# Gate and up as seven block products by halves of the tokens, in a gated cross-attention and FFN kernel

## The reference, cut to what matters

```python
x = x + tanh(g_xattn) * xattn(layernorm(x), ctx)          # 32 heads, 8 K/V groups, head size 16
h = layernorm(x)                                          # 2048 tokens x 512
g, u = h @ gate.T, h @ up.T                               # 2048 shared and 256 routed rows each
shared = (g * sigmoid(g) * u)[:, :2048] @ sh_down.T
routed = (g * sigmoid(g) * u)[:, 2048:] @ r_down.T * comb_w   # comb_w: softmax over the two best of 8 logits
x = x + tanh(g_ffn) * (shared + routed)
```

## Time and profile before

| | |
|---|---|
| median of 3 runs | 1016.08 us |
| the profiled execution | 1011.93 us |
| its span | 1010.2 us, so 1.7 us lie around it |
| granted TensorE clock, mean | 0.971 |
| busy in the span | PE 959.4, DVE 518.2, ACT 317.2, POOL 139.6 us |
| attention up to the first FFN product | 0 to 404.69 us |
| FFN | 404.69 us to the end |

### The profile page before, as it was taken

The page is one execution under the profiler, slowest core; times in us unless marked ns, Lnnn a source line. Parts: engine busy times, 40 slices in busy tenths (PEclk is TensorE's granted clock), DMA queues, the critical chain, the costliest instruction groups (busy, mean ns, idle before and its releaser), DMA issues.

```text
span 1010.2 us, 14045 instructions
## 1 busy us (share of the span) xinstructions
PE 959.4 (95%) x5108; PEld 745.0 (74%) x5108; DVE 518.2 (51%) x876; ACT 317.2 (31%) x587; POOL 139.6 (14%) x65
## 2 busy tenths in 40 slices
PE   4689999989998798999999999999999999999998
PEld 4556666766675565888888888888888888778887
DVE  7688777768777795542424242333324242423333
ACT  5165556547545366531111111011111111102110
POOL 4213001300300310400300203003030030120000
PEclk9789999989998799999999999999999999999999
DMA  7774343434334611100100100001001000000012
GB/s 260 168 147 101 70 112 62 92 74 89 81 82 90 172 33 65 63 1 1 63 0 1 63 1 21 41 0 62 0 0 62 0 0 0 1 1 1 1 56 112
DMA packets 33276, 56.71 MB, mean 56 GB/s; under 512 B 4304, under 2 KB 20176, under 8 KB 31824
## 3 DMA queue, kind: packets, MB, share of 16 engines
q1 hardware_dynamic: 33232, 56.13, 21.2%
HBM read 41.17 MB, written 14.68 MB: 55 GB/s over the span
## 4 chain that ended last, share of the span: by engine, by line
PE 73%; issue 17%; DVE 4%; DMA 3%; POOL 2%; ACT 1%; SPq 0%; POOLq 0%; DVEq 0%; ACTq 0%
PE bank L983 22%; PE bank L984 21%; PE bank L985 21%; PE bank L1058 3%; PE bank L1038 2%; PE bank L1048 2%; DVE mcol L695 1%; PE bank L988 1%; POOL xa L392 1%; DMA q_scr<-qx_l 1%; POOL cx_l L361 1%; PE bank L1274 1%; DMA wfc_raw<-wfc 1%; DMA xa<-x 1%; DMA q_st<-q_scr 0%
## 5 line engine op out<-in xcount | busy, mean ns | idle before, releaser
L950 DVE TENSOR_TENSOR hid<-bank,silu 128x512 f32<-128x512 f32 x72 | 49.8, 692 | 353.3 <-ACT silu L652 353.3
L983 PE MATMUL bank<-x2T_l,w_h 128*128 128x512 f32 x576 | 225.3, 391 | 0.0
L985 PE MATMUL bank<-x2T_h,w_h 128*128 128x512 f32 x576 | 224.6, 390 | 0.0
L984 PE MATMUL bank<-x2T_h,w_l 128*128 128x512 f32 x576 | 224.6, 390 | 0.0
L695 DVE TENSOR_REDUCE mcol<-bank 128x2 f32<-128x512 f32 x256 | 170.3, 679 | 59.4 <-PE bank L1038 58.7
L579 ACT ACTIVATE probs<-bank 128x512 f32<-128x512 f32 x256 | 149.6, 594 | 147.3 <-PE bank L1048 146.6
L652 ACT ACTIVATE silu<-bank 128x512 f32<-128x512 f32 x72 | 43.1, 599 | 482.5 <-PE bank L985 482.5
L1038 PE MATMUL bank<-k_st,q_st 65*128 65x256 f32 x512 | 116.2, 316 | 25.1 <-DMA q_st<-q_scr 14.9
L1038 PEld LDWEIGHTS bank<-k_st,q_st 65*128 65x128 f32 x512 | 95.3, 206 | 58.6 <-issue 21.3
L983 PEld LDWEIGHTS bank<-x2T_l,w_h 128*128 128x128 f32 x576 | 108.5, 188 | 23.8 <-issue 0.8
L984 PEld LDWEIGHTS bank<-x2T_h,w_l 128*128 128x128 f32 x576 | 108.6, 188 | 22.4
(11 more groups left out here) (108 smaller groups left out, 933.5 us busy)
## 6 DMA issues: line engine op xcount, KB each, us to landing
w_raw<-w_ffn SPq DMA_DIRECT2D x9, 1536.0 KB, 6.6
q_st<-q_scr SPq DMA_DIRECT2D x96, 128.0 KB, 3.8
xa<-x SPq DMA_DIRECT2D x4, 1024.0 KB, 8.4
cx_raw<-ctxT SPq DMA_DIRECT2D x16, 256.0 KB, 3.4
q_scr<-qx_h SPq DMA_DIRECT2D x16, 256.0 KB, 2.1
q_scr<-qx_l SPq DMA_DIRECT2D x16, 256.0 KB, 2.5
out<-xa SPq DMA_DIRECT2D x16, 256.0 KB, 2.0
k_st<-k_scr SPq DMA_DIRECT2D x24, 128.0 KB, 3.9
```

Of the source, the lines that this page charges most:

```text
L950: v.tensor_tensor(hid[:, ic, :], bank[2 * ic + 1][:, :], silu[:, ic, :], ALU.mult).then_inc(hid_ok, 1)
L983: mm(out, a_h, b_l, start=start, stop=False)
L984: mm(out, a_l, b_h, start=False, stop=False)
L985: return mm(out, a_h, b_h, start=False, stop=stop)
```

## The change

Gate and up of one chunk of 128 rows are now read as one product of 2 x 2 blocks. The left side has the gate chunk in the first row and the up chunk in the second, each cut into two halves of the 512 inputs (A11, A12 and A22, A21). The right side has the same two halves of the inputs by two runs of 512 tokens. In Winograd's form of Strassen's method this takes seven block products of 128 x 256 by 256 x 512 rather than eight, with sums of blocks of the weights (S1 to S4) and of the tokens (T1 to T4) ahead, and sums of the products behind.

The tokens are done in two halves of 1024; the weights are loaded and split anew for each half. In a half there are 18 chunks (quads), in pairs; G = 0 to 35 counts quads, M = 0 to 17 pairs. In each pair the down products of the pair before (8 tiles, 48 matmuls) stand in the first quad between its fourth and fifth product. PE has 36 x 42 matmuls for gate and up where it had 36 x 48; down is as before, 864.

POOL now makes for every quad the four sums S (128 x 256 each), the cast and the subtraction of seven blocks (128 x 1792), and those of the down weights (128 x 512). In the last block of attention it also makes the T sums and splits the token blocks of the first half. ACT copies the turned tiles to `xs0` there. The second half's tiles are prepared between the halves (`turn`, `x7_high` on ACT, `x7_low` on DVE, `differences` on POOL). DVE makes u2, u3, c22, c21, c12 from PSUM and a tile in SBUF, and `hid0`, `hid1` from two tiles in SBUF.

```diff
+TERMS = {1: (A11, B11), 2: (A12, B21), 3: (S4, B22), 4: (A22, T4), 5: (S1, T1), 6: (S2, T2), 7: (S3, T3)}
@@ POOL
-            def split_w(sc, par):
-                    pool.wait_ge(y_full, TILES * BLOCKS * (sc - 1))
-                g.tensor_copy(w_h[par][:, :], w_raw[:, par, :]).then_inc(ffn_w_hi, 1)
-                g.tensor_tensor(w_l[par][:, :], w_raw[:, par, :], w_h[par]..., ALU.subtract).then_inc(ffn_w_ok, 1)
+            def split_gu(G, f):
...
+                    pool.wait_ge(full[3], G - 1)
+                pool.wait_ge(sums, 4 * G + 4)
+                g.tensor_copy(w_h[f][:, :, :], raw[f][:, 0:7, :]).then_inc(gu_hi, 1)
+                pool.wait_ge(gu_hi, G + 1)
+                g.tensor_tensor(w_l[f][:, :, :], raw[f][:, 0:7, :], w_h[f][:, :, :].bitcast(f32),
+                                ALU.subtract).then_inc(gu_ok, 1)
+            def pair(half, m):
+                split_gu(2 * M + 1, 1)
+                block_sums(2 * M + 2, 0, True)
+                for f in range(2):
+                    split_dn(2 * M + f, f, M)
...
+                split_gu(2 * M + 2, 0)
+                block_sums(2 * M + 3, 1, True)
@@ ACT, in the last block of attention
+                if half == 0 and k >= 2:
+                    act.wait_ge(x7_ok, k // 2)
+                copy(lot.rearrange("p a k -> p (a k)"), source[:, :]).then_inc(x2_cp, 1)
@@ ACT, a quad
+                copy(r1[:, :], bank[0][:, :]).then_inc(r1_ok, 1)
+                high(G - 1, M, 1 - f, 1)
+                nc.scalar.activation(s0[:, :], bank[0][:, :], ACT.Silu).then_inc(s0_ok, 1)
+                high(G, M, f, 0)
+                nc.scalar.activation(s1[:, :], c12[:, :], ACT.Silu).then_inc(s1_ok, 1)
@@ DVE, a quad
+                add(u2[:, :], bank[1], r1).then_inc(u2_ok, 1)
+                h_low(G - 1, 1 - f, 1)
+                dve.wait_ge(full[7], G + 1)
+                add(u3[:, :], bank[1], r1).then_inc(u3_ok, 1)
+                accumulate(half, M - 1, range(HTILES), False)      # first quad of a pair
+                add(c22[:, :], bank[2], u3).then_inc(c22_ok, 1)
+                add(c21[:, :], bank[3], u3).then_inc(c21_ok, 1)
+                v.tensor_tensor(hid0[:, :], c21[:, :], s0[:, :], ALU.mult).then_inc(hid_ok[0], 1)
+                dve.wait_ge(full[3], G + 1)
+                add(c12[:, :], bank[2], u2).then_inc(c12_ok, 1)
+                h_low(G, f, 0)
+                dve.wait_ge(s1_ok, G + 1)
+                v.tensor_tensor(hid1[:, :], c22[:, :], s1[:, :], ALU.mult).then_inc(hid_ok[1], 1)
@@ PE, a quad
+                product(1, f, bank[0], False)
+                product(6, f, bank[1], False)
+                pe.wait_ge(r1_ok, G + 1)
+                product(2, f, bank[0], True)
+                pe.wait_ge(u2_ok, G + 1)
+                product(7, f, bank[1], True)
+                if f == 0 and not is_at(m, 0):
+                    down(half, M - 1)
+                product(5, f, bank[2], False)
+                product(4, f, bank[3], False)
+                pe.wait_ge(c22_ok, G + 1)
+                product(3, f, bank[2], True)
```

More of the change, by code:

```diff
@@ L352, in _ @@
+            for half in range(HALVES):
+                pair(half, 0)
+                with sp.Fori(1, PAIRS - 2) as m:
+                    pair(half, m)
+                pair(half, PAIRS - 2)
+                pair(half, PAIRS - 1)
             sp.wait_ge(stored, 16 * (T // P))
@@ new lines, in x7_high, with pair @@
+            def x7_high(j):
+                act.wait_ge(t_ok, 4 * (TILES + j) + 4)
+                act.wait_ge(full[3], FBLOCKS)
+                hi = x7_h[:, :, :, :].rearrange("p a c q -> p (a c) q")[:, :, j * P:(j + 1) * P]
+                copy(hi, xs[j % 2][:, 1:8, :].rearrange("p a (c q) -> p (a c) q", c=2)).then_inc(x7_hi, 1)
+            def pair(half, m):
+                M = PAIRS * half + m
+                turn = half == 0 and is_at(m, PAIRS - 1)
+                quad(2 * M, M, 0, not is_at(m, 0), turn)
+                quad(2 * M + 1, M, 1, True, turn)
+                if is_at(m, 0):
+                    act.wait_ge(comb_ok, 5 * half + 1)
+                    nc.scalar.activation(comb[:, 1, :], comb[:, 0, :], ACT.Tanh, scale=0.5).then_inc(e_ok, 1)
+                if is_at(m, PAIRS - 1):
+                    high(2 * M + 1, M, 1, 1)
+                if turn:
+                    x7_high(0)
+                    x7_high(1)
+                    for k in range(4, 8):
+                        x2_copy(1, k, bank[TURN_BANKS[k - 4]])
+                        if k == 6:
+                            x7_high(2)
+                    x7_high(3)
@@ L665, in _ @@
+            pairs(act, pair)
         @block.vector
@@ L1279, in logits_turn, with product @@
-            def logits_turn(k):
-                pe.wait_ge(lg_cp, 1)
-                pe.wait_ge(acc_ok, TILES * k + 2)
+            Y = bank[4:8]
+            def product(k, f, to, onto):
+                a, b = TERMS[k]
+                for c in range(2):
+                    w = slice(c * P, (c + 1) * P)
+                    last = three(to[:, :], w_h[f][:, a, w], w_l[f][:, a, w], x7_h[:, b, c, :], x7_l[:, b, c, :],
+                                 not onto and c == 0, c == 1, onto)
+                last.then_inc(full[k], 1)
@@ new lines, in turn, with pair @@
+            def turn():
+                for k, ready in zip(range(4, 8), (u3_ok, s0_ok, c21_ok, c12_ok)):
+                    pe.wait_ge(ready, FBLOCKS)
+                    x2_job(1, k, bank[TURN_BANKS[k - 4]])
+            def pair(half, m):
+                if is_at(m, 0):
+                    pe.wait_ge(x7_ok, TILES * (half + 1))
+                quad(half, m, 0)
+                quad(half, m, 1)
+                if is_at(m, PAIRS - 1):
+                    M = PAIRS * half + m
+                    if half == 0:
+                        pe.wait_ge(x2_cp, HTILES + 4)
+                    down_open(M)
+                    if half == 0:
+                        turn()
+                    down_close(M)
+                    if half == 0:
+                        pe.wait_ge(x2_cp, T // P)
@@ L1315 @@
+            for half in range(HALVES):
+                pair(half, 0)
+                pair(half, 1)
+                with pe.Fori(2, PAIRS - 1) as m:
+                    pair(half, m)
+                pair(half, PAIRS - 1)
 _OUT = (B, S, D)
```

719 lines of the change are left out of this document (429 added, 290 removed).

## The result

| | before | changed |
|---|---|---|
| median | 1014.65 us (4 runs, 1008.13 to 1019.41) | 1186.12 us (4 runs, 1180.24 to 1190.51) |
| ratio | | 1.168, 95% interval 1.162 to 1.174 |
| profiled execution, its span | 1011.93, 1010.2 us | 1180.24, 1178.5 us |
| granted TensorE clock, mean | 0.971 | 0.912 |
| PE busy in the span | 959.4 us | 985.5 us |

What follows compares the result with a forecast made beforehand. PE's count of matmuls was taken to bound the FFN. From the profiled span, 1010.2 - 49 + 9 + 1 + 13 = 984; + 115 + 73 = 1172; + 1.7 around the span = 1174 us, range 985 to 1200.

Steps and rivals of the forecast that it cites:

- fewer matmuls: FFN gate and up on PE: 36 quads lose 6 matmuls each, 216 x 0.2267 = 49.0 us less.
- idle for each quad, u2 the releaser: FFN loop, before product 7: PE waits 3.5 us for DVE's u2 in 33 quads, 115 us.
- clock: FFN loop: PE's clock falls to half speed after each idle, costing 2.2 us, 33 times, 73 us.
- a pair: FFN loop: two quads with their down products take 41 us if the collision occurs in every quad.
- loop stall and clock: FFN loop: PE's idles before product 7 and the clock's falls after them, 115 + 73 us.
- attention's last block: End of attention: POOL's new work, waits and transposes, less a split no longer made there, net +13 us.
- the turn: Between the two token halves: preparing the second half's tiles outlasts the down products, 9 us (5 to 13).
- the end: Very end of the kernel: the last low part is ready later than the covering down matmuls end, 1 us.
- loads: FFN weights loaded twice, 27 MB rather than 14, with DMA queues 8% busy: no cost.
- the opening of the FFN: Start of the FFN loop: the prediction had no term for a wait there.
- hid1: Sign in the FFN quads: DVE's hid1 averages 3 us or more, hid0 and the low parts under 1.5.
- who goes first: FFN quad: POOL's waiting subtraction precedes hid1, 3.5 us idle; rival, DVE first, 999 us, chance 0.22.

Runs made afterwards that it cites:

- experiment 1: The changed kernel, but c21, hid0, c12, its silu and hid1 made in place in PSUM banks, so no quad operation of DVE has two SBUF inputs: 1024.14 us.
- experiment 5: Kernel of experiment 1, second half's roots made behind the third quad's split and that quad's weight load issued earlier: 1012.57 us; roots alone 1012.64 us.
- experiment 3: The changed kernel with POOL's subtraction of 1792 columns cut into seven pieces of 256: 1046.92 us, ratio 1.019.
- experiment 4: The changed kernel with DVE's order alone changed, the low part of hid0 made behind the next quad's u2: 1112.20 us, ratio 1.083.
- experiment 6: Kernel of experiment 5 with DVE, ACT and POOL work reordered around the turn: first kernel 997.82 us; second, with two more order changes, 991.69 us.
- experiment 2: The changed kernel with c12 and its silu kept in PSUM and only hid1 read from a bank, written to SBUF: 1085.08 us, ratio 1.056.

## Why the prediction was right

By its own steps, prediction against the profile of the changed kernel:

| step | predicted | measured |
|---|---|---|
| fewer matmuls | -49.0 us | a pair of 132 matmuls takes 29.92 us in experiment 1, 132 x 0.2267 |
| idle for each quad, u2 the releaser | 33 x 3.5 us | 31 x 3.55 (109.9 us) |
| clock | 2.2 us a quad | 1.6 us |
| a pair | every 41 us | 40.77 us |
| loop stall and clock | 115 + 73 = 188 us | 31 x (40.77 - 29.92) / 2 = 168 us |
| attention's last block | +13 us | +10.2 (first FFN product at 414.88, not 404.69) |
| the turn | 9 us | 14.1 us |
| the end | 1 us | 0.98 us |
| loads | 0 | no wait of PE in the FFN is put down to a load; POOL waited for one for 11.6 us at the opening, where moving it won nothing (experiment 5) |
| the opening of the FFN | not seen | 10.5 us |
| hid1 | 3 us or more, the others under 1.5 | 3.9 in the mean; 1.2 the low parts, 1.0 hid0 |

- **What was right** is the sequence: the quad shown runs as it was worked out, and experiments 1, 3 and 4, each from another side, take most or all of the wait away from hid1. That the total came so near is in part luck, as the errors below show, and the range was so wide that it took in a gain as well.
- **The main choice was who goes first** when both engines wait, with only an operation of 0.24 us to go by the earlier trace rows. It was the operation issued first, at 4 us too. The Trainium skill (SBUF — State Buffer, Who interferes with whom) says "Issue order, not op shape, decides who blocks"; hid1 at 4478 ns behind the subtraction and at 797 ns ahead of it (experiment 4) agree.
- **Slightly off:** the subtraction is recorded as 4.32 rather than 4.05 us because it is issued while it still waits for the low part; undisturbed it takes 3.95 (at 450.78, above).
- **The turn was mis-sized**, 14.1 for 9 (idles of 0.56, 3.17 and 10.40). The last low part for the tokens, taken as at most 2.4 us, took 5.77, behind POOL's subtraction for quad 19. I had the rule and did not apply it to this operation. From the timelines of DVE and PE, the tokens' last two low parts and PE's first product of the second half:

```profile
800.75 2.03 DVE L1149 TENSOR_TENSOR x_l<-xs,x_h 128x1792 fp32r<-128x1792 f32 x1 [1.94 <-ACT x_h L576]
...
807.28 5.77 DVE L1149 TENSOR_TENSOR x_l<-xs,x_h 128x1792 fp32r<-128x1792 f32 x1 [3.19 <-ACT x_h L576]
```

```profile
813.16 0.77 PE L1186 MATMUL bank<-x_l,w_h 128*128 128x512 f32 x1 [10.40 <-issue]
```

- **The opening was missed.** The prediction counted what POOL does there, and not what POOL waits for: 9.12 us for DVE's statistics, ahead of a split that is due. The forecast of 1172 for the span came out only 6.5 below 1178.5, because the errors partly cancel: loop 20 and attention 3 too high, turn 5 and opening 10.5 too low, and nothing was put down for the clock behind those two, 2.2 us at the opening and 5.4 at the turn (from the matmuls at half speed there). Some 6 us are not accounted for. The attention's 3 is itself the difference of two executions, and the table above shows how far these differ.
- **A condition that was too narrow.** I wrote of operations with two SBUF inputs. Two of 8 columns, the first in the kernel of experiment 1, the second in the first one of experiment 6, show more (timelines of DVE):

```profile
677.36 3.96 DVE L1096 TENSOR_SCALAR comb<-comb 128x8 f32<-128x8 f32 x1
```

```profile
661.37 3.95 DVE L964 SCALAR_TENSOR_TENSOR nmr<-mv,rstd 128x8 f32<-128x8 f32 x1
```

The first has one tile as input. Such an operation takes 0.16 us once POOL's subtraction is over (the next one, at 681.23); here it took 4 us of DVE, and PE was idle for 4.1 before product 7, the three small operations behind it included.

## What to carry to other kernels

A DVE operation with two inputs in SBUF, and here also a TENSOR_SCALAR with one, that finds POOL in a long instruction waits for what is left of that instruction, and what hangs behind it on DVE's queue pays as well. Before moving work to an idle POOL, list DVE's operations without a PSUM operand in the same stretch; leave intermediate tiles in their bank (in place), or cut POOL's instruction into pieces of the length that the schedule can bear. Taking one operation out of the collision, or moving it, hands the wait to the next one (experiments 2 and 4). With the loop repaired alone the seven-product form was still 0.9% slower than eight products (0.5 to 1.3%); its 4% came with the order at the opening and the turn, and with the pieces and the signal in attention's last block.

## What was not expected of the hardware

- **Small operations wait too; a transpose and a statistic did not.** The TENSOR_SCALAR of 8 columns with one SBUF input waited for 3.96 us. But with POOL's subtraction under way from 366.31 to 370.39 in the first kernel of experiment 6, a transpose and a batch-norm statistic, both from SBUF to SBUF, took their usual time (timelines of POOL and DVE). The Trainium skill (SBUF — State Buffer, Who interferes with whom) names operations with two SBUF inputs and those of a two-port mode; that the TENSOR_SCALAR was in such a mode no run here shows.

```profile
366.31 4.08 POOL L502 TENSOR_TENSOR x_l<-xs,x_h 128x1792 fp32r<-128x1792 f32 x1
```

```profile
366.55 0.45 DVE L985 STREAM_TRANSPOSE aT<-oN 128x256 f32<-128x256 f32 x1
...
368.75 0.68 DVE L883 BATCH_NORM_STATS2 stats<-xa 128x6 f32<-128x512 f32 x1
```

- **The clock did not fall at every idle.** Behind 25 of the 31 idles for u2 or u3, 7 to 14 matmuls ran at half speed (1.2 GHz), which cost 1.5 to 3.0 us each time. Behind four idles of the same length (those before 529.36, 652.30, 850.23 and 1037.95) none did, and behind those before 437.98 and 836.36 only two. The quad shown above is one of the four; here are its first matmuls behind the idle, 0.24 us apart, and then those behind the next idle, 0.43 apart (timeline of PE):

```profile
652.63 0.39 PE L1187 MATMUL bank<-x_h,w_l 128*128 128x512 f32 x1
652.87 0.39 PE L1188 MATMUL bank<-x_h,w_h 128*128 128x512 f32 x1
...
665.60 0.80 PE L1186 MATMUL bank<-x_l,w_h 128*128 128x512 f32 x1 [3.48 <-DVE u L1057]
666.19 0.63 PE L1187 MATMUL bank<-x_h,w_l 128*128 128x512 f32 x1
666.62 0.63 PE L1188 MATMUL bank<-x_h,w_h 128*128 128x512 f32 x1
```

- **Idles of 1.89 us went with a lower clock, idles of 0.67 us didn't.** In experiment 3, with idles of 0.33 and 0.67 us in each pair, the clock stayed at 1.00; in experiment 2, with 1.89 and 0.31, it was 0.96 (the same stretch of both, columns as above). A pair of experiment 2 cost 4.5 us more than one of experiment 1, of which 2.2 are shown as idle and 0.5 are not shown, so some 1.8 went to the clock, by subtraction.

```profile
460.00:700.00 240.00, 230.71 (x991) 183.64 (x990) 167.00 (x197) 45.42 (x79) 187.81 (x209) 1.00 0.15 48
```

```profile
460.00:700.00 240.00, 225.90 (x934) 180.03 (x933) 175.47 (x183) 41.31 (x72) 160.62 (x114) 0.96 0.15 46
```

- **POOL's wait is recorded as its work.** Its operations behind a DVE operation are longer by what they wait (the first of the sums 1.18 rather than 0.73 us), so a POOL total can't be taken from such rows.
